# The closing of row 31 in an attention stage: the order of the last instructions, the PSUM banks of row 31's output, and the last store in two parts

## What is computed

```
x = x + layer0(x)      # gated causal averages, a blend of traces, a projection, a layer norm
x = x + layer1(x)      # attention, 16 heads of 8 channels over 128 keys
# layer1, for each row of the batch:
Q, K, V = proj(Wq), proj(Wk), proj(Wv)
scores  = einsum('bhqd,bhkd->bhqk', Q, K) * scale        # plus a bias that depends on the row
out     = softmax(scores) @ V                            # dense, or over 32 gathered keys
return out @ Wo.T + bo
```

## Time and profile before

| what | us |
|---|---|
| median of 3 runs | 363.81 (363.51 to 364.02) |
| profiled execution, its own time | 363.04 |
| its span, first to last instruction | 361.3 |
| TensorE busy | 314.9 (87%) |
| VectorE busy | 294.0 (81%) |
| GpSimd busy | 232.8 (64%) |
| ScalarE busy | 213.1 (59%) |
| last result of VectorE ends | 357.90 |

### The profile page before, as it was taken

The page is one execution under the profiler, slowest core; times in us unless marked ns, Lnnn a source line. Parts: engine busy times, 40 slices in busy tenths (PEclk is TensorE's granted clock), DMA queues, the critical chain, the costliest instruction groups (busy, mean ns, idle before and its releaser), DMA issues. The chain is left out here.

```text
span 361.3 us, 10349 instructions
## 1 busy us (share of the span) xinstructions
PE 314.9 (87%) x3361; PEld 214.1 (59%) x3361; DVE 294.0 (81%) x1530; ACT 213.1 (59%) x452; POOL 232.8 (64%) x281
## 2 busy tenths in 40 slices
PE   1869559998999989898938499899999999999994
PEld 0426227564564746564523366677888877787782
DVE  4865998879697878879684876799999999999961
ACT  5733302575546363554704557878887888887772
POOL 3045143563745455563733397699999999999980
PEclk9969788999999999999977879999999999999998
DMA  7101000100000045200552055545644564301011
GB/s 218 37 0 32 0 0 2 30 4 29 2 4 27 3 88 79 37 0 0 77 71 30 1 77 79 136 110 73 131 109 112 85 128 102 82 3 34 3 32 30
DMA packets 23473, 18.91 MB, mean 52 GB/s; under 512 B 2304, under 2 KB 23040, under 8 KB 23424
## 3 DMA queue, kind: packets, MB, share of 16 engines
q1 hardware_dynamic: 23424, 18.31, 25.6%
HBM read 3.62 MB, written 2.10 MB: 16 GB/s over the span
## 5 line engine op out<-in xcount | busy, mean ns | idle before, releaser
L1415 POOL TENSOR_TENSOR arena<-arena,neg_max 128x512 f32<-128x512 f32 x128 | 130.2, 1057 | 20.0 <-DVE neg_max L1289 19.8
L1289 DVE CUSTOM_DVE_ANT_0 arena<-ps,arena 128x128 f32<-128x128 f32 x512 | 113.8, 286 | 10.7 <-issue 5.4
L938 ACT ACTIVATE arena<-ps 128x512 f32<-128x512 f32 x128 | 69.7, 596 | 16.7 <-PE ps L673 16.7
L673 PE MATMUL ps<-ident_sb,arena 128*128 128x128 f32 x512 | 69.1, 279 | 0.0
L673 PEld LDWEIGHTS ps<-ident_sb,arena 128*128 128x128 f32 x512 | 57.0, 142 | 6.8 <-POOL arena L1415 3.8
L1375 POOL TENSOR_TENSOR arena<-arena 128x448 f32<-128x448 f32 (+6 forms) x56 | 39.9, 712 | 30.8 <-DVE arena L1117 28.4
L1362 POOL TENSOR_TENSOR arena<-decay_a,arena 128x192 f32<-128x192 f32 x32 | 22.3, 720 | 40.3 <-ACT arena L798 40.3
L1289 DVE DVE_READ_ACCUMULATOR2_ANT neg_max<- 128x1 f32 x512 | 42.5, 83 | 0.0
L689 PE MATMUL ps<-arena 128*32 128x128 f32 x1024 | 41.7, 281 | 0.0
L1117 DVE TENSOR_TENSOR arena<-ps,arena 128x448 f32<-128x448 f32 (+6 forms) x56 | 23.6, 427 | 16.3 <-PE ps L460 9.6
L659 PE MATMUL ps<-arena 48*128 48x128 bf16 x512 | 26.1, 223 | 5.5 <-DVE neg_max L1289 5.4
(11 more groups left out here) (154 smaller groups left out, 594.0 us busy)
## 6 DMA issues: line engine op xcount, KB each, us to landing
arena<-q_parts SPq DMA_DIRECT2D x96, 64.0 KB
arena<-k_parts SPq DMA_DIRECT2D x96, 64.0 KB
arena<-in_x SPq DMA_DIRECT2D x8, 256.0 KB, 2.9
out<-arena SPq DMA_DIRECT2D x8, 256.0 KB, 3.2
w_sb<-in_w SPq DMA_DIRECT2D x1, 576.0 KB, 5.8
arena<-in_consts SPq DMA_DIRECT2D x1, 420.0 KB, 4.4
rows_sb<-in_rows SPq DMA_DIRECT2D x1, 288.5 KB, 2.9
ident_sb<-in_ident SPq DMA_DIRECT2D x1, 64.0 KB, 2.7
```

Source lines behind the costliest of these rows:

```text
L673: mm = pe.transpose(ps[1][:, q % 2, k * P:k * P + P], neg_t[q % NT_RING][:, k * P:k * P + P], ident)
L938: act.activation(probT[q % PT_RING], ps[1][:, q % 2, :], ACT.Exp, scale=-1.0)\
L1289: dve.tensor_tensor_reduce(out=neg_t[q % NT_RING][:, cs], in0=ps[0][:, score_bank(c) + slot, cs], in1=nbias[n % 2], scale=1.0, scalar=3.0e ...
L1415: pool.tensor_tensor(t4, t4, neg_max[:, n % 2, 4 * z:4 * z + 4].unsqueeze(2).broadcast_to([P, 4, P]), ALU.subtract).then_inc(s["shifted"], 1)
```

## The change

It touches only the closing calls, the banks of row 31's output and the last store. Nothing in the loop over the octets changes, except that its functions ask `out_bank` for the bank, which for rows 0 to 30 is the same as before. Row 31's output is written to `ps[0]` instead: what `turn_o` writes to its bank 0, what `turn_attn` writes to bank 1, what `project` writes to bank 2. `turn_o(31)` waits for the last `logits` (`negt_ready` 512) instead of the row before.

```
+        def out_bank(n, k):
+            return ps[0][:, k, :] if n == B - 1 else ps[1][:, 3, :]
...
-            for g in range(G - 3, G):
+            for g in range(G - 3, G - 1):
                 store(g)
+            last = (G - 1) * GB
+            sp.wait_ge(s["y_ready"], last + GB - 1)
+            sp.dma_start(out_v[:, last:last + GB - 1, :], yout[(G - 1) % 2][:, 0:GB - 1, :]).then_inc(s["y_stored1"], 16)
+            sp.wait_ge(s["y_ready"], last + GB)
+            sp.dma_start(out_v[:, last + GB - 1:last + GB, :], yout[(G - 1) % 2][:, GB - 1:GB, :])\
+                .then_inc(s["y_stored1"], 16)
             sp.wait_ge(s["y_stored0"], 16 + 16 * G // 2)
-            sp.wait_ge(s["y_stored1"], 16 + 16 * G // 2)
+            sp.wait_ge(s["y_stored1"], 32 + 16 * G // 2)
...
             def turn_o(n):
-                if n == 0:
+                if n == B - 1:
+                    pe.wait_ge(s["negt_ready"], 8 * 2 * B)
+                elif n == 0:
...
             over_octets(octet_step)          # TensorE
+            values(2 * B - 1)
             turn_attn(B - 2)
-            values(2 * B - 1)
+            turn_o(B - 1)
             project(B - 2)
-            turn_o(B - 1)
             turn_attn(B - 1)
             project(B - 1)
...
             over_octets(octet_step)          # ScalarE
+            move_o(B - 1)
             move_attn(B - 2)
-            move_o(B - 1)
             move_attn(B - 1)
...
             over_octets(octet_step)          # VectorE
+            normalise(B - 1)
             result(B - 2)
-            normalise(B - 1)
             result(B - 1)
```

More of the change, by code:

```diff
@@ L703, in turn_o @@
                 for o in range(2):
-                    mm = pe.transpose(ps[1][:, 3, o * P:o * P + P], oT[n % 2][:, o * P:o * P + P], ident)
+                    mm = pe.transpose(out_bank(n, 0)[:, o * P:o * P + P], oT[n % 2][:, o * P:o * P + P], ident)
                 mm.then_inc(s["on_ps"], 1)
@@ L708, in turn_attn @@
                 pe.wait_ge(s["attn_ready"], n + 1)
-                pe.transpose(ps[1][:, 3, 2 * P:3 * P], attn[n % 2], ident).then_inc(s["attnT_ps"], 1)
+                pe.transpose(out_bank(n, 1)[:, 2 * P:3 * P], attn[n % 2], ident).then_inc(s["attnT_ps"], 1)
             def project(n):
                 pe.wait_ge(s["attnT_ready"], n + 1)
-                pe.matmul(ps[1][:, 3, 3 * P:4 * P], attnT[n % 2], wt["wo"], start=True, stop=True).then_inc(s["y_ps"], 1)
+                pe.matmul(out_bank(n, 2)[:, 3 * P:4 * P], attnT[n % 2], wt["wo"], start=True, stop=True).then_inc(s["y_ps"], 1)
             def octet_step(c):
@@ L948, in move_attn @@
                 act.wait_ge(s["attnT_ps"], n + 1)
-                act.activation(attnT[n % 2], ps[1][:, 3, 2 * P:3 * P], ACT.Copy).then_inc(s["attnT_ready"], 1)
+                act.activation(attnT[n % 2], out_bank(n, 1)[:, 2 * P:3 * P], ACT.Copy).then_inc(s["attnT_ready"], 1)
             def octet_step(c):
@@ L1295, in normalise @@
                 dve.wait_ge(s["on_ps"], n + 1)
-                o = ps[1][:, 3, 0:2 * P].rearrange("p (h e) -> p h e", e=2 * DH)
+                o = out_bank(n, 0)[:, 0:2 * P].rearrange("p (h e) -> p h e", e=2 * DH)
                 dve.reciprocal(rden[:, n % 2, :], o[:, :, DH]).then_inc(s["rden_ready"], 1)
@@ L1311, in result @@
                     dve.wait_ge(s[f"y_stored{g % 2}"], 16 * (g // 2 + 1))
-                dve.tensor_tensor(yout[g % 2][:, b, :], ps[1][:, 3, 3 * P:4 * P], x1b_all[:, n, :], ALU.add)\
+                dve.tensor_tensor(yout[g % 2][:, b, :], out_bank(n, 2)[:, 3 * P:4 * P], x1b_all[:, n, :], ALU.add)\
                     .then_inc(s["y_ready"], 1)
```

## The result

The changed kernel took 360.85 us (median of 6 runs, 360.31 to 361.49), the kernel before 363.97 us (6 runs, 363.51 to 365.44). The ratio is 0.991, 95% interval 0.989 to 0.993: faster by about 3.1 us, where 1.6 was forecast, and outside the forecast's range of 361.35 to 363.0. The profiled execution took 361.49 us, with a span of 359.7 us.

What follows compares the result with a forecast made beforehand. The prediction took the end to be bound by row 31's serial steps, waiting for row 30's bank, then the last store. Gains 0.93 + 0.70 = 1.63 us off the 363.81 median gave 362.2 us, range 361.35 to 363.0.

Steps and rivals of the forecast that it cites:

- row 30's steps hidden: Closing: row 30's moved steps, now behind row 31's, would be off the path and cost 0.
- the three-row store landed unseen: Last store: rows 28 to 30, issued at about 355.75, would land before row 31's store ends; cost 0.
- The store's term: Last store in two parts: a gain of 0.7 us, from bounds of 0.2 to 1.3.
- The 1.6 us for a row's landing: Row 31's 64 KB store: lower bound from issue to landing, 2.3 − 0.71 = 1.6 us, against 2.9 for four rows.
- the trickle: End of the last store before the change: single packets after the bulk, about 0.6 us, which might come again in full.
- The hand-over from `move_o(31)` to `turn_o(31)`, 0.04: Closing: `oT` ready at 354.34, `turn_o(31)` starting at about 354.38, with the logits wait already passed.
- its 0.25: Gap before `turn_o(31)` in the kernel before, read as the price of one wait that is its own instruction, on `y_ready`.
- the order and the banks: Closing: `values(63)` and `move_o(31)` earlier, row 31 in its own bank; `turn_o(31)` starts 0.93 us earlier.
- The runs' own spread 0.25: Low end of the range: 361.6 less 0.25 us for the spread of the runs, giving 361.35.
- The slower rival: Row 31's store runs on few of 16 DMA engines; kernel 1.3 us slower, 365.1; chance 0.04.
- rival 1: Last store: row 31's store takes as long as the four-row store, landing 2.9 behind issue; 362.9; chance 0.12.
- Rival 2: Closing: own wait delays `turn_o(31)` (0.25 lost) or `values(63)` is held (0.43 lost); 0.25 to 0.5 left, about 363.0; chance 0.08.

Runs made afterwards that it cites:

- e7: Kernel before, with the last four-row store issued about 1.1 us later, behind an added GpSimd addition that waits for result(31); 365.09 us in one profiled run.
- c0: Kernel before, unchanged, run again for a second profile and more runs; median 364.11 us of 12 runs, ratio 0.9996.
- e1: Changed kernel with its last four rows in one store again, order and banks still changed; median 362.47 us, ratio 0.9962.
- e3: Kernel before, with only `values(63)` put ahead of `turn_attn(30)`; 363.95 us in one profiled run.
- e6: Changed kernel with the last store cut into two rows and two rows instead of three and one; 361.21 us in one profiled run.

## Why the prediction was wrong, point by point

The direction, the main mechanism and each place were right: `values(63)` 0.59 us behind `values(62)` (forecast 0.6), `move_o(31)` 0.72 behind that (0.71), no stall from row 30, row 30's steps hidden, the three-row store landed unseen, the row's bytes on all engines. Three sizes were off.

1. *The store's term, "I take 0.7".* This is the step of the sum that failed. It was 1.33 (2.87 to 1.54). The 1.6 us for a row's landing was right. What was wrong is the sentence that nothing tells why the trickle came: the trace held the packet of queue 14, and the rate of 379 GB/s in the slice where it lies. The forecast read the sum over the queues and not each queue. This is 0.6 us.

2. *The hand-over from `move_o(31)` to `turn_o(31)`, 0.04.* It was 0.14. The forecast took the last wait in the code, the one for `oT`, to be part of the transpose, and let the wait for the logits pass behind `turn_attn(30)` for nothing. The trace has it the other way round: the wait for `oT` is the instruction of its own, it comes when `move_o(31)` has ended, and it costs 0.10. The kernel before showed this already, in L702 behind L701; for the same reason its 0.25 was not the price of one wait but of two. So the order and the banks gave 0.82 and not 0.93. With both terms corrected the sum is 0.82 + 1.33 = 2.15 us, and 363.81 − 2.15 = 361.7, inside the range: the two sizes made the forecast too small, by 0.5 us together, but did not take it out of its range.

3. *"The runs' own spread 0.25."* This took the result out of the range. It was read from three runs, 0.5 us apart. The runs of this kernel go over 4.4 us, for the larger part with the clock ahead of the closing, and the profile of before did show two stretches of 40 us at a mean clock of 0.79. By the trace 2.1 of the measured 3.1 are the change, and about 1 is the draw: the same program run again gave 1.5. That the first comparison came out at 3.1 is luck, and so is the 1.5, which is as near to the forecast 1.6 as the first was far.

The slower rival (the row on few engines) and rival 1 (landing without regard to size) are out: 1.5 us and a burst of the full rate. Rival 2's wait of its own did fall on `turn_o(31)`, at 0.10 and not 0.25; its "0.25 to 0.5 of the 0.93" is the case of both losses or of the second alone, and the first alone would have left 0.68.

## What to carry to other kernels

When the last item waits for a buffer of the one before, give it a buffer of its own first: a reordering alone can lose what it gains afterwards. Where an instruction needs two waits, look in the trace which of them stands alone: one on the critical path cost 0.10 us here, and dropping a wait that another one implies removed it. Split the last store so that only the last piece's bytes stand behind the last result, and look at the DMA queues there one by one: another queue's packet on one engine can hold up the whole landing. And before a gain of a microsecond is read from medians, see how much the mean clock of the runs differs, or count from a mark in the trace that lies behind the disturbance.

## What the runs showed of the hardware that was not expected

- One packet of an instruction queue occupies one DMA engine for 0.3 us alone (e7) and 0.5 to 0.7 us among a store's packets (before, c0, e1, e3, e6). A store whose bytes are in motion then lands 0.5 to 0.8 us later (2.8 to 3.1 instead of 2.3 for 256 KB; 2.6 where 1.85 was expected for 128 KB).
- Of two waits ahead of `turn_o(31)`, the one written last and met last became the instruction of its own, and the one met long before was carried by the transpose. Each such instruction behind the release cost 0.10 to 0.11 us: the hand-over was 0.04 us with none, 0.14 with one, 0.24 to 0.25 with two.
- The same program differs by up to 4.4 us from run to run. Two thirds of that variance go with the mean granted clock, 1.6 us for each 0.01, and the clock differs in two stretches in which TensorE has gaps.
